# Soft-mixture logits as three fp32r products of high and low halves

## Reference, cut to what matters

```
x = _layernorm(x, norm_g, norm_b)
se = _layernorm(slot_embeds, slot_g, slot_b) * scale
logits = jnp.einsum('bnd,esd->bnes', x, se)
dispatch = jax.nn.softmax(logits, axis=1)
combine = jax.nn.softmax(logits.reshape(B, N, -1), axis=-1)
slots = jnp.einsum('bnd,bnes->besd', x, dispatch)
```

## Time and profile before

| | us |
|---|---|
| median of three runs | 1034.99 |
| lowest, highest | 1034.04, 1036.65 |
| the profiled execution | 1035.9 |
| its span, first to last instruction | 1034.2 |
| PE busy in the span | 930.6 (90%) |
| DVE busy | 729.3 (71%) |
| POOL busy | 571.2 (55%) |
| ACT busy | 527.9 (51%) |

### The profile page before, as it was taken

One profiled execution on the slowest core, in us unless ns is written; L12 is line 12 of the kernel. 1 busy time (PEld: TensorE's weight loads), 2 busy tenths in 40 slices (PEclk: granted clock), 3 DMA queues, 4 the chain that ended last, 5 costly groups with the idle time before them and its releaser, 6 DMA issues.

```text
span 1034.2 us, 15582 instructions
## 1 busy us (share of the span) xinstructions
PE 930.6 (90%) x4453; PEld 709.0 (69%) x4453; DVE 729.3 (71%) x1692; ACT 527.9 (51%) x1028; POOL 571.2 (55%) x566
## 2 busy tenths in 40 slices
PE   5699799899988799999999999999996879968696
PEld 3477667566678576788888888888874746646474
DVE  7677477799935478766666666666666778886865
ACT  2244456644581435666666666666661334443264
POOL 6111244477742126677777777777773339984600
PEclk9899799999999889999999999999997669998798
DMA  6000000022200000000000000000002000000001
GB/s 183 1 1 1 1 2 1 21 82 62 65 6 26 1 9 1 22 25 25 26 25 23 23 23 25 28 23 23 24 3 102 1 0 1 1 1 0 1 11 31
DMA packets 27110, 23.96 MB, mean 23 GB/s; under 512 B 3419, under 2 KB 23987, under 8 KB 26803
## 3 DMA queue, kind: packets, MB, share of 16 engines
q1 hardware_dynamic: 27059, 23.34, 7.6%
HBM read 22.28 MB, written 1.05 MB: 23 GB/s over the span
## 4 chain that ended last, share of the span: by engine, by line
PE 80%; DVE 13%; POOL 3%; ACT 2%; issue 1%; DMA 1%; SPq 0%; DVEq 0%; ACTq 0%; POOLq 0%
PE psum L1758 74%; PE psum L1872 1%; DVE stats L1231 1%; PE psum L1828 1%; PE psum L1777 1%; POOL rstd L605 1%; DVE xn L1244 1%; DVE arena L1317 1%; PE psum L1949 1%; ACT arena L812 1%; DVE mv L1234 1%; DMA wq<-in_wq 1%; POOL xn L610 1%; POOL xn L611 1%; DVE arena L1340 0%
## 5 line engine op out<-in xcount | busy, mean ns | idle before, releaser
L1758 PE MATMUL psum<-xw 128*128 128x512 f32 x1392 | 367.6, 397 | 5.1 <-DVE xw L1404 2.6
L1758 PEld LDWEIGHTS psum<-xw 128*128 128x128 f32 x1392 | 260.6, 189 | 64.2 <-issue 8.5
L663 POOL TENSOR_TENSOR hh<-arena,hh 128x512 fp32r<-128x512 f32 x176 | 228.1, 1296 | 82.2 <-ACT hh L812 80.8
L1758 PE MATMUL psum<-hh,wdn 128*128 128x512 f32 x672 | 196.8, 398 | 7.0 <-ACT hh L812 3.5
L1566 DVE TENSOR_TENSOR psum<-psum,arena 128x512 f32<-128x512 f32 x176 | 123.2, 700 | 104.0 <-PE psum L1758 97.7
L812 ACT ACTIVATE hh<-arena 128x512 fp32r<-128x512 f32 x228 | 143.1, 629 | 46.2 <-DVE arena L1688 43.1
L1033 ACT ACTIVATE arena<-psum 128x512 f32<-128x512 f32 x176 | 105.2, 598 | 119.7 <-PE psum L1758 119.6
L1758 PEld LDWEIGHTS psum<-hh,wdn 128*128 128x128 f32 x672 | 126.2, 189 | 47.9 <-POOL hh L708 16.3
L1758 PE MATMUL psum<-arena 128*128 128x18 f32 (+7 forms) x776 | 121.4, 315 | 10.8 <-ACT arena L812 7.5
L1571 DVE TENSOR_TENSOR arena<-psum,arena 128x512 f32<-128x512 f32 x176 | 121.7, 692 | 7.7 <-DVE psum L1566 1.7
L1758 PEld LDWEIGHTS psum<-arena 128*128 128x128 f32 (+3 forms) x776 | 93.4, 192 | 26.3 <-issue 16.2
(11 more groups left out here) (288 smaller groups left out, 1431.7 us busy)
## 6 DMA issues: line engine op xcount, KB each, us to landing
egu<-in_w SPq DMA_DIRECT2D x44, 128.0 KB, 2.1
egu<-in_egu SPq DMA_DIRECT2D x16, 256.0 KB, 2.6
edn<-in_w SPq DMA_DIRECT2D x44, 64.0 KB, 1.8
edn<-in_edn SPq DMA_DIRECT2D x16, 128.0 KB, 2.0
arena<-in_w SPq DMA_DIRECT2D x1, 1536.0 KB, 6.8
X<-in_x SPq DMA_DIRECT2D x4, 256.0 KB, 3.8
arena<-in_conv SPq DMA_DIRECT2D x1, 1024.0 KB, 9.0
out<-X SPq DMA_DIRECT2D x4, 256.0 KB, 2.3
```

Source lines behind the costliest of these rows:

```text
L663: pool.tensor_tensor(hh[:, s % 4, 1, :], h1[:, s % 2, :], hh[:, s % 4, 0, :].bitcast(F32), ALU.subtract).then_inc(hh_lo, 1)
L1758: return pe.matmul(dst, lhsT=lhsT, rhs=rhs, start=start, stop=stop)
```

## The change

Each logits matmul becomes the three fp32r products high x high, high x low and low x high. ACT writes the slot embeddings and the tokens of L == 1 twice, once as float32 and once as the fp32r high half (into `hh` and `xall`). POOL subtracts to get the low halves: both slot groups and token groups 0 to 2 after its four `ln_power`, and token group 3 ahead of step 4 of its loop. PE waits for the new semaphore `logits_lo` ahead of each logits step.

```diff
+        def slot_half(ch, half):
+            return hh[:, ch // 4, half, P * (ch % 4):P * (ch % 4) + P]
@@ POOL, L == 1, behind ln_power(1, 0..3)
+                    def tokens_low(g):
+                        pool.wait_ge(ln_xnT, NG + g + 1)
+                        pool.tensor_tensor(norm_half(g, 1), xnT[:, 512 * g:512 * g + 512], norm_half(g, 0).bitcast(F32), ALU.subtract)\
+                            .then_inc(logits_lo, 1)
+
+                    for g in range(2):
+                        pool.wait_ge(se_T, g + 1)
+                        pool.tensor_tensor(hh[:, g, 1, :], seT[:, 512 * g:512 * g + 512], hh[:, g, 0, :].bitcast(F32), ALU.subtract)\
+                            .then_inc(logits_lo, 1)
+                    for g in range(NG - 1):
+                        tokens_low(g)
                     for k in range(4 * B):
+                        if k == 4:
+                            tokens_low(NG - 1)
                         pool.wait_ge(brec_done, k + 1)
@@ ACT, ln_evac_group
-                    ins = act.activation(dst, bank(6 + g % 2), ACT.Identity, scale=cols[:, COL["norm_g"]:COL["norm_g"] + 1],
-                                         bias=cols[:, COL["norm_b"]:COL["norm_b"] + 1])
+                    for into in (dst, norm_half(g, 0)):
+                        ins = act.activation(into, bank(6 + g % 2), ACT.Identity, scale=cols[:, COL["norm_g"]:COL["norm_g"] + 1],
+                                             bias=cols[:, COL["norm_b"]:COL["norm_b"] + 1])
@@ ACT, slot embeddings
-                        act.activation(seT[:, 512 * g:512 * g + 512], bank(g), ACT.Identity, scale=slot_gs[:, 0:1], bias=slot_gs[:, 1:2])\
-                            .then_inc(se_T, 1)
+                        for into in (seT[:, 512 * g:512 * g + 512], hh[:, g, 0, :]):
+                            last = act.activation(into, bank(g), ACT.Identity, scale=slot_gs[:, 0:1], bias=slot_gs[:, 1:2])
+                        last.then_inc(se_T, 1)
@@ PE, logits_slots
+                pe.wait_ge(logits_lo, 2 + b // 2 + 1)
                 for c in range(2):
-                    ch = 2 * j + c
-                    last = mm(psum[:, k % 3, N * c:N * c + N], seT[:, P * ch:P * ch + P], xnT[:, N * b:N * b + N])
+                    last = product(psum[:, k % 3, N * c:N * c + N], lambda h: slot_half(2 * j + c, h), lambda h: xall[:, h, N * b:N * b + N])
```

More of the change, by code:

```diff
@@ L342, in build_program @@
         least_done = sem("least_done")
+        logits_lo = sem("logits_lo")
         least_mm = sem("least_mm")
```

## The result

The changed kernel takes 1039.37 us (median of 9 runs, 1037.55 to 1040.59) where the kernel before takes 1034.99 (median of 9). The ratio is 1.0036, with 95% interval 1.0024 to 1.0047: slower by 2.5 to 4.9 us. By the ratio's centre it is 3.7 us, by the two medians 4.4. The profiled execution took 1039.02, its span is 1037.3 (before 1034.2).

What follows compares the result with a forecast made beforehand. PE was taken as the bound of the logits stage, a chain of engines as the start's. +7.45 - 0.39 + 0.57 - 0.4 + 0.2 - 4.5 = +2.9 us gave 1037.9 against the median 1034.99; range 1033.5 to 1042.0.

Steps and rivals of the forecast that it cites:

- Rival A: The forecast itself: the start loses 7.4 us, the logits stage gains 4.5, giving 1037.9; chance 52%.
- The record of 256 fp32r columns: Steady logits stage: a record costs 0.117 us, six cost 0.70 instead of four at 0.87, gaining 0.165 a step.
- Rival B: Logits products: weight loads stand in line with streams, 0.215 us a record, +19.2 in all, 1054.2; chance 5%.
- PE stays last: Steady steps: the chain DVE, POOL, PE has 0.42 us of room, falling by 0.165, so PE remains the bound.
- ACT's copy late by 0.63: Attention's tail: ACT's second slot writes delay its copy of PE's output by 0.63 us.
- The 16 attention records, +0.4: Behind ACT's copy: pushed by 0.63, their last third falls under the low clock, adding 0.4 us, bounds 0 and 0.8.
- POOL's halves ahead of the first logits, +7.45: Start: first logits wait for POOL's group 3 chain plus three subtractions, 126.4 instead of about 118.9 us.
- From there to step 0's transposes, -0.39 and +0.57: Start at low clock: logits 0 take 0.39 us less; group 3 transposes and logits 1 and 2 take 0.57 more.
- Token group 3 ahead of step 4, +0.2: POOL's extra subtraction there comes 0.34 us late against some 0.15 of room, costing 0.2, bounds 0 and 0.5.
- The stage, -4.7: Logits stage: 27 steps save 0.165 us each (4.5), logits 3 save 0.4, token group 3's subtraction costs 0.2.
- rival C: Start: high clock speeds logits 1 and 2, then step 0's transposes and logits 3 by another 1.2 us; 1032.8; 12%.
- rival D: Start costs more, including 3.4 us more at half clock in steps 0 to 2 (+1.7); +5.5, 1040.5; chance 25%.

Runs made afterwards that it cites:

- two_products: The changed kernel without the third product (low slots x high tokens), so logits less exact; 1032.01 us, 0.9975 of the kernel before.
- slot_writes_split: The changed kernel with ACT's float32 slot writes moved behind the copy PE waits for in the attention's tail; 1038.86 us, 1.0034 of the kernel before.
- slots_early: The changed kernel with POOL's two slot low halves made ahead of its group 3 chain instead of behind it; 1037.28 us, 1.0023 of the kernel before.

## Why the prediction was right, step by step

The forecast was 1037.9 and a loss of 2.9 us; measured are 1039.37 and 4.4, with an interval of 2.5 to 4.9 that holds both 2.9 and the distance's 3.05. Rival A happened: the start loses more than the stage gains. Three terms missed by 0.5 to 1.0 us, in both directions, so it is in part luck that the sum comes this close.

- **The record of 256 fp32r columns: right.** 0.117 was taken. In the step shown, six logits records put their end 0.70 us behind the end of the transposes (160.29 + 0.95 less 159.94 + 0.60): 0.117 each. By tile one of them lasts 283 ns (median of 192), and (0.95 - 0.28)/5 = 0.134 between starts; the first starts sooner beside the transposes than an fp32 one does (0.35 us after them, 0.44 before), so the distance between starts alone would read too high. 25 steps from 142.23 to 192.40 are 2.007 us each, forecast 2.00, before 2.161: 0.154 a step instead of 0.165. That the trace of before held no such matmul did not matter: a row with as many loads and half the columns did. The Trainium skill, on the page TensorE: Matmul & The Clock Gate, Part 3, "What overlaps and what doesn't", says that loads overlap only when the row group differs; taken alone, that sentence would have had these full loads stand between the streams. The trace disagrees: six loads take 0.77 us (from 160.26) within the 0.95 of the products (from 160.29). Rival B falls with the step's 2.007 (it gave 2.58).
- **PE stays last: right.** two_products shows that the other chains let a step of 1.77 us pass.
- **ACT's copy late by 0.63: right.** PE waits 1.03 for it instead of 0.37 ahead of the same instruction, +0.66. slot_writes_split takes it away, and the 1.03 and 0.37 are the same in every profile with and without the double write.
- **The 16 attention records, +0.4: mis-sized.** They took 2.72 instead of 1.86, +0.86. I let a third of them fall under the low clock, and a third of 1.86 us at half the clock is 0.6 and not 0.4. The rest is scatter: 1.86 to 2.96 us without the delay, 2.40 to 3.44 with it. It is the widest scatter that I found in one place.
- **POOL's halves ahead of the first logits, +7.45: right.** From tile 14's transpose to the first logits it is 7.88 us before and 15.64 after, +7.76, which is the forecast and the 0.46 that the attention records had more, less 0.15 in small pieces. The first logits were forecast at 126.4 and start at 126.43; that this fits to 0.03 is luck, because tile 14's transpose came 0.44 sooner in this profile and the attention records took 0.46 more. slots_early moves two of the three subtractions out and gets 2.44 of it back.
- **From there to step 0's transposes, -0.39 and +0.57: right in sum.** It is 9.12 us before and 9.26 after, +0.14 where +0.18 was forecast. Transposes and logits 1 and 2 take 3.68 us (129.95 to 133.63), forecast 3.85.
- **Token group 3 ahead of step 4, +0.2: too much.** It makes POOL's next multiplication 0.22 late and not 0.34, and there is that much room: PE waits in neither place, so it costs 0.
- **The stage, -4.7 (27 steps -4.5, logits 3 -0.4, group 3 +0.2): right in sum, wrong in its parts.** It is -4.85. From the logits of step 5 to those of step 31 are 26 of the 27 steps, -3.68 and not 26 x 0.165 = -4.3: 26 x 0.154 are 4.0, and the first of them took 2.33 us because the clock was still low. From step 0's transposes to step 1's it is -1.40, where -0.4 was forecast: the clock was up there for a moment (0.91 from 133 to 137; before, 0.51 until 131.2), which is the second half of rival C. From step 1's transposes to the logits of step 5 it is +0.23, at a clock of 0.52 from 137 to 140.4, which is a part of rival D. The forecast had no term for either. Nor is it fixed: the same transposes take 0.66 us in the changed kernel and 1.12 in slot_writes_split, where they come 1.5 us sooner.
- **Open: the whole against the trace.** By the medians the loss is 4.4 us, by the ratio 3.7, by distance 3.05 or 2.2. The median of the kernel before alone moved between 1034.58 and 1035.91 from session to session, and behind the stage each of two pieces falls into one of two groups 1.5 to 2 us apart, in both kernels. Whether the change adds anything behind the stage stays open; the interval allows either.

The chances leaned to slower by over 0.3% with 0.51 against 0.41 for within it; the result is 0.36%, near that edge, for the reasons given: two pieces on opposite sides, one of 8 us and one of 5.

## What to carry to other kernels

An operand made ahead of a product has two prices, its own time and its place: here six subtractions of some 1.24 us each cost nothing on an engine that is idle nearly half the time, except for the three that the first product waits for and that were put behind the last thing to become ready, and except where two of them meet DVE's normalisation. Before making a stage's products cheaper, follow the new operand back from the first product, in the queue order of the engine that makes it, and put it where its inputs are ready. And an idle time of PE can be paid twice, once as such and once by the low clock that it leaves in place; two matmuls that nobody reads, one in each of two waits, bought 2.5 us here.

## What the runs showed of the hardware that I had not expected

- Four 128x128 fp32 TENSOR_SCALAR instructions of DVE take 1.11 us alone and 2.50 beside POOL's 128x512 subtractions; a single one went from 0.34 to 1.30 us, about the length of one subtraction (1.24). POOL's two were not slowed (2.49 against 2.51). The Trainium skill, in the GPSIMD Engine Reference, Section 1, "Specifications", says that GpSimd shares its SBUF interfaces with VectorE and contends with DVE instructions that run in a 2-port performance mode or have two SBUF inputs. The trace agrees in that the meeting shows, and only on DVE's side; in which mode DVE ran these instructions no trace here shows.
- Filler matmuls in a wait brought the clock up: with four of them, most of which ran at 0.50, the stretch after the wait ran at 1.00 instead of 0.50 and took 2.09 us instead of 3.68. They didn't delay the product behind them, which started 3.86 us behind POOL's first subtraction, against 3.85.
- Two long pieces of unchanged code each fall into one of two groups (229 or 231 us, 114 or 115 to 116), so a span of 1034 us scatters by some two microseconds. A piece of 1 us is read from a distance within one stage, not from the whole time.
